# Moving the probability-times-value matmuls one product forward in a two-layer gated cross-attention kernel

## What is computed

```python
# layer 0, for each batch (16 heads of 32)
q = layernorm(x) @ Wq.T + bq ; k = ctx @ Wk.T + bk ; v = ctx @ Wv.T + bv
scores = clip(q @ k.T / sqrt(32), -50, 50)      # masked, clipped again
probs = softmax(scores) ; probs /= probs.sum() + 1e-8
heads = probs @ v
# layer 1, linear attention, from the same ctx
k1, v1 = split(ctx @ Wkv.T) ; k1 = where(k1 > 0, k1 + 1, exp(k1))
kv_summary = k1.T @ v1 ; k_sum = k1.sum()
```

## Time and profile before

| | |
|---|---|
| median of 3 runs | 1098.64 us (1098.49 to 1098.93) |
| profiled execution, its own time | 1097.97 us |
| its span | 1096.4 us |
| TensorE matmul busy | 998.6 us, 91% of the span |
| VectorE busy | 495.7 us, 45% |
| ScalarE busy | 286.3 us, 26% |
| chain that ended last | TensorE 78%, VectorE 12%, ScalarE 4% |
| mean granted TensorE clock | 0.965 of full speed |

### The profile page before, as it was taken

One profiled execution on the slowest core, in us unless ns is written; L12 is line 12 of the kernel. 1 busy time (PEld: TensorE's weight loads), 2 busy tenths in 40 slices (PEclk: granted clock), 3 DMA queues, 4 the chain that ended last, 5 costly groups with the idle time before them and its releaser, 6 DMA issues.

```text
span 1096.4 us, 14784 instructions
## 1 busy us (share of the span) xinstructions
PE 998.6 (91%) x5711; PEld 772.2 (70%) x5712; DVE 495.7 (45%) x885; ACT 286.3 (26%) x436; POOL 102.0 (9%) x127
## 2 busy tenths in 40 slices
PE   4799999999999999877999999998999999999980
PEld 4687878778878888655999744897898445555640
DVE  5444546464646464897222144897431412122123
ACT  4422423333323233542221111433220001111100
POOL 1100000000000000210000000312000411211215
PEclk9899999999999999988999999999889999999995
DMA  8000000000000000730000200811600516977616
GB/s 326 1 1 29 1 29 28 2 31 1 29 1 29 1 1 1 288 134 1 1 1 1 115 0 1 322 64 51 237 1 1 195 57 222 326 248 248 221 46 201
DMA packets 25690, 95.79 MB, mean 87 GB/s; under 512 B 3234, under 2 KB 4258, under 8 KB 22434
## 3 DMA queue, kind: packets, MB, share of 16 engines
q1 hardware_dynamic: 18162, 69.01, 17.6%
q0 software_dynamic: 7472, 25.96, 6.7%
HBM read 76.35 MB, written 18.61 MB: 87 GB/s over the span
## 4 chain that ended last, share of the span: by engine, by line
PE 78%; DVE 12%; ACT 4%; issue 4%; DMA 1%; POOL 1%; DVEq 0%; POOLq 0%; ACTq 0%; SPq 0%
PE ps L498 16%; PE ps L499 16%; PE ps L500 16%; PE ps L862 9%; PE ps L730 6%; PE ps L872 5%; PE ps L838 3%; PE ps L577 3%; PE ps L750 1%; DVE zinv L1316 1%; POOL arena L1731 1%; DVE stats L1206 1%; DVE queries_l L1197 1%; ACT arena L1004 1%; ACT queries_h L915 1%
## 5 line engine op out<-in xcount | busy, mean ns | idle before, releaser
L498 PE MATMUL ps<-arena_r 128*125 128x512 f32 (+1 forms) x416 | 158.0, 380 | 16.6 <-DVE arena_r L1183 10.5
L499 PE MATMUL ps<-arena_r 128*125 128x512 f32 (+1 forms) x416 | 157.8, 379 | 0.0
L500 PE MATMUL ps<-arena_r 128*125 128x512 f32 (+1 forms) x416 | 157.4, 378 | 0.0
L498 PE MATMUL ps<-hT,arena_r 128*128 128x448 f32 (+1 forms) x368 | 139.3, 379 | 3.1 <-DVE hT L1222 1.9
L499 PE MATMUL ps<-hT,arena_r 128*128 128x448 f32 (+1 forms) x368 | 137.2, 373 | 0.0
L500 PE MATMUL ps<-hT,arena_r 128*128 128x448 f32 (+1 forms) x368 | 136.8, 372 | 0.0
L862 PE MATMUL ps<-arena 128*128 x336 | 103.1, 460 | 1.6 <-ACT arena L1152 1.0
L498 PEld LDWEIGHTS ps<-arena_r 128*125 128x125 f32 (+1 forms) x416 | 78.4, 189 | 31.9 <-DVE arena_r L1183 10.2
L1305 DVE TENSOR_SCALAR arena<-ps 125x1344 f32<-125x1344 f32 x32 | 49.8, 1555 | 87.2 <-PE ps L500 87.2
L1004 ACT ACTIVATE arena<-arena,mbias,mscale 125x448 f32<-125x448 f32 x84 | 57.9, 753 | 116.5 <-DVE arena L1305 111.2
L500 PEld LDWEIGHTS ps<-arena_r 128*125 128x125 f32 (+1 forms) x416 | 78.1, 188 | 13.5
(11 more groups left out here) (194 smaller groups left out, 1362.1 us busy)
## 6 DMA issues: line engine op xcount, KB each, us to landing
arena<-in_e SPq DMA_DIRECT2D x16, 1408.0 KB, 6.8
arena<-in_e SPq DMA_DIRECT2D x16, 512.0 KB, 8.8
sorted_rows<-arena POOLq DMA_DIRECT2D x1, 7424.0 KB, 24.5
land_c<-in_ctx SPq DMA_DIRECT2D x8, 752.0 KB, 4.4
arena<-sorted_rows POOLq DMA_DIRECT2D x21, 256.0 KB, 6.4
sorted_rows<-arena POOLq DMA_DIRECT2D x21, 256.0 KB, 6.0
land_w<-in_gu SPq DMA_DIRECT2D x8, 512.0 KB, 11.6
arena<-in_e SPq DMA_DIRECT2D x16, 192.0 KB, 9.2
```

Source lines behind the costliest of these rows:

```text
L498: mm(into, a[0], w[0], start=i == 0, stop=False)
L499: mm(into, a[0], w[1], start=False, stop=False)
L500: last = mm(into, a[1], w[0], start=False, stop=i == len(operands) - 1)
```

## The change

Each mix moves forward by one product in TensorE's list; nothing else moves. For groups 0 to 2 it comes between the `k1` and the `v1` product of `values`, and for group 3 between the third and the fourth `keys_T`. The last batch's own list, and all other engines' lists, stay as they are.

```diff
-            def values(b, c):
+            def values(b, c, between=None):
...
+                    if j == 2 and between is not None:
+                        mix(*between)
                     product(ps[0:TP, bank, :], [(piece(ctxT, k, c * TP, TP), piece(w, k, first, D))
...
                     if g < 3:
-                        values(b + 1, g)
+                        values(b + 1, g, between=(b, slot, g))
                     else:
                         for gg in range(G):
                             keys_T(b + 1, gg)
-                    mix(b, slot, g)
+                            if gg == 2:
+                                mix(b, slot, g)
```

## The result

| | before | after |
|---|---|---|
| median | 1098.57 us (1096.07 to 1098.93, 4 runs) | 1113.86 us (1109.84 to 1115.22, 4 runs) |
| ratio | | 1.0138, 95% interval 1.0108 to 1.0168 |
| profiled execution, its span | 1097.97, 1096.4 us | 1109.84, 1108.3 us |

The changed kernel is 15.3 us slower by the medians; 14.9 were predicted.

The account below looks back on a forecast made before the run. TensorE was taken to bound the kernel, held at batch ends by VectorE's chain. Mechanical 8.6 us (7.4 + 0.5 + 0.75) plus 6.3 for clock falls gave 14.9 over 1098.64: 1113.5 us, range 1106.5 to 1116.5.

Parts of the forecast that it names:

- What bounds: Attention stage: no mix waits for exponentials; TensorE waits at batch ends, five times for kv_save, 5.9 us in all.
- Groups 0 to 2 cost nothing: Mixes of groups 0 to 2 ahead of the v1 product: cost 0, with about 1.05 us of slack in group 0.
- The fourth keys product slides by 1.48 us: Group 3: product, eviction, context rounding and VectorE's chain come 1.48 us later; five boundary gaps grow to 2.62, costing 7.4 us.
- `kv_summary` hides the extra switch: At kv_summary the 0.31 us wait becomes about 0.2 and absorbs the extra switch; cost 0.
- The loop's turn, 0.5 us: Boundary where the loop turns: v0 has 0.96 us of slack against 1.48 us of delay, so 0.5 us remains.
- The last boundary, 0.75 us: Last boundary, without a summary: the fourth keys' low part ends later and the scores wait 0.75 us for it.
- The clock, 4 x 1.58: Behind four of the five 2.6 us boundary gaps the clock falls to half, 1.58 us each, 6.3 us in all.
- Sum: Whole kernel: mechanical 8.6 us plus clock 6.3 us make 14.9 us more.
- A: Rival at the batch boundaries: the clock holds at most of them, only the mechanical part comes, 1107.3 us; chance 0.28.
- C: Rival at VectorE's normalise: it waits for mix 3, so an earlier mix makes the kernel faster, 1092.7 us; chance 0.02.
- B: Rival in the batch: something else takes up the delay, nearly no change, 1099 to 1104 us; chance 0.04.
- D: Rival at group 0's mix: the exponentials are late, 3.5 us added over seven batches, 1117 us; chance 0.03.

Follow-up runs that it names:

- two filled ones: Changed kernel with nine unread score matmuls issued again in TensorE's boundary gaps, at every boundary (ratio 1.0122) or except at the loop's head (1.0140), against the kernel before.
- filled kernel: Changed kernel, TensorE's loop kept, with group 0's nine score matmuls issued again into free bank 5 in the boundary gaps; at every boundary 1.0122 to the kernel before.
- written-out kernel: Changed kernel with TensorE's loop over batches 1 to 4 written out, gaps not filled; ratio 1.0143 to the kernel before.
- with the gaps filled and the loop written out: Changed kernel with TensorE's loop written out and nine unread score matmuls issued again at all six boundaries; ratio 1.0079 to the kernel before.
- the save first: VectorE's kv_save put ahead of normalise(b, 1): on the kernel before 0.9943, with the loop written out too 0.9927, on the changed kernel 1.0043.

## Why the prediction was right, step by step

- **What bounds.** Right. In the batches that the change touches no mix waited, before or after; the end of VectorE's chain held TensorE.
- **Groups 0 to 2 cost nothing.** Right (1.0016), and the slack of 1.05 us too: one product further the waits appeared, within 0.2 us of the lengths that follow from it.
- **The fourth keys product slides by 1.48 us.** Measured: gaps of 2.63 to 2.74 us instead of 1.14 to 1.23, 1.49 to 1.52 more at each boundary, and batches of 52.6 instead of 51.1 us. Right to 0.04 us.
- **`kv_summary` hides the extra switch.** Right: its wait shrank from 0.31 to about 0.1 us; I had said 0.2, so the slack was a little smaller than read.
- **The loop's turn, 0.5 us.** If the fall of the clock there is taken at 1.56 us, 54.5 - 1.56 - 52.4 leaves 0.6, so the number fits; but that is luck. I had the late end of VectorE's chain use up the slack and hold `v0` for the last 0.5 us. The changed kernel shows no such wait:

```profile
246.64 0.44 PE L498 MATMUL ps<-queries_h,arena_r 128*125 128x448 f32 x1 [2.21 <-issue]
...
248.69 0.16 DVE L1295 COPY ks<-ps 128x2 f32 x1
...
249.76 0.63 PE L498 MATMUL ps<-arena_r 128*125 128x512 f32 x1
...
251.29 0.50 PE L500 MATMUL ps<-arena_r 128*125 128x512 f32 x1 [0.56 <-issue]
```

  The bank was free at 248.69 + 0.16 = 248.85, and `v0` started at 249.76, behind scores that ran at half clock. What grew were two stalls of TensorE's own: at the turn from 1.96 to 2.21 us, and about a dozen matmuls later from 0.17 to 0.56, together 0.64 more. And I excluded a fall at this place, where one came. In all six looped kernels with group 3's mix moved, the turn's stall is 2.06 to 2.49 us and a fall follows (in the two filled ones only behind the second stall, of 1.92 and 1.31 us); in the five with that mix in its old place it is 1.60 to 1.96 and none does. Why the earlier mix lengthens the stall stays open.
- **The last boundary, 0.75 us.** Measured: 55.84 us (filled kernel, no fall) against 53.55, less the 1.48 of the ordinary boundary in the same distance: 0.81.
- **The clock, 4 x 1.58.** Four falls, 1.56 us each, though three of them at the five ordinary gaps and one at the turn. The count was right by two errors that cancelled: four of five was one too many in the profiled execution. That a gap of 2.6 us doesn't always bring a fall I had only assumed; 5 of 6 in the written-out kernel and 3 of 5 here bear it out. My reading that the cases part near 2 us does not hold, though. Behind the attention stage, where the earlier trace rows show a fall after 2.08 us, the kernel with groups 0 to 2 moved idles just as long before the same matmul, and its clock stays up (timeline, then the stretch behind):

```profile
454.63 0.50 PE L498 MATMUL ps<-arena_r,hT 128*128 128x512 f32 x1 [2.08 <-DVE arena_r L1181]
```

```profile
454.80:458.20 3.40, 2.85 (x13) 2.01 (x14) 1.24 (x1) 2.12 (x4) 2.17 (x2) 1.00 1.02 410
```

  At this place ten of the fourteen profiles have a gap of 2.02 to 2.28 us, and in five of them the clock falls. So the length of one gap doesn't settle it, and the count of falls was a matter of luck within the range that I gave.
- **Sum.** The stage lost 15.15 us: 6.2 for the clock at 1.56 per fall, and 8.9 that remain as mechanical, where 6.3 and 8.65 stood. The median moved by 15.3.
- **Rivals.** A (the clock holds) gave 1107.3 us; with the gaps filled and the loop written out that is what is measured (1.0079, 1098.6 x 1.0079 = 1107.3 us). It wasn't the case, since at 2.6 us most gaps do bring a fall. C was refuted by the changed kernel itself: `normalise` followed `context_low` as before, though the mix had by then been over for 5.9 us. B has fallen with the ratio. D doesn't arise in this change and does with the save first.
- **Where it was too confident.** The spread of the kernel before is wider than its three runs showed: 1095.6 to 1103.8 us over 20 runs on one chip. The 0.2% that I took for the least difference to be told from none needed several rounds.

## What to carry to other kernels

When an operation is moved earlier on the busiest engine, ask what it was covering where it stood: work behind which another engine's chain runs is free, and in front of the product that starts the chain it is a delay in full. A free move can be free only because something else is late; with the save first, the slack that had made one free was used up (by the estimate above), so measure again after such a mending. Judge such a change by the distance between like points of a repeated stage, which here separates effects of 1.5 us from a remainder of the program that varies by 10.

## What the runs showed of the hardware

- Idle gaps on TensorE of 2.6 to 2.75 us in the attention stage were followed by 3.4 us at half clock in most cases: 3 of 5 in the changed kernel, 5 of 6 with the loop written out. Lone gaps of up to 1.96 us brought none there. The loop's turn had a fall in all six kernels whose stall was 2.06 to 2.49 us; in the two filled ones it came only behind a second stall, of 1.92 and 1.31 us. Right behind the stage, gaps of 2.02 to 2.28 us brought one in five of ten profiles. Each fall in the stage costs some 1.56 us, with the engine busy behind it.
- The section "HAM oscillation — how this bites in real kernels" of the Trainium skill's page "TensorE: Matmul & The Clock Gate" warns only of idle gaps longer than these. The trace doesn't agree: the clock fell behind gaps of 2.21 to 2.74 us in the changed kernel, and at 1.56 us each its four falls are 6.2 of the 15.15 us.
- Useless matmuls can pay: 54 of them in six gaps took 0.6% off the time.
- The turn of TensorE's loop costs 2.7 us here (a batch of 52.49 us against 49.76 with the loop written out, the save first in both). With matmuls added to the loop a second stall behind the turn grew from 0.56 us to 1.92 (added at its head too) and 1.31 (added elsewhere only). Why was not tried.
